# Padding the expert lists page by page during the token loop, and reading the expert rows back two tiles at a time

## What is computed

```python
x = x + attention(layernorm(x), ctx, valid_lens, Wq, Wk, Wv, Wo)
u = layernorm(x)
s = softmax(u @ centroids.T + expert_biases)
vals, idx = top_k(s, 2)                       # two experts a token
g = scatter(vals, idx)                        # 16 gates a token, 14 of them zero
routed = sum_e g[e] * (u @ Wr[e].T + br[e])
shared = (sum_n u @ Ws[n].T + sum_n bs[n]) / 2
out = x + u + routed + shared
```

## Time and profile before

| | us |
|---|---|
| median of 3 runs | 261.77 (260.43 to 262.01) |
| the profiled execution: its time | 261.29 |
| its span | 259.4 |

### The profile page before, as it was taken

The page is one execution under the profiler, slowest core; times in us unless marked ns, Lnnn a source line. Parts: engine busy times, 40 slices in busy tenths (PEclk is TensorE's granted clock), DMA queues, the critical chain, the costliest instruction groups (busy, mean ns, idle before and its releaser), DMA issues.

```text
span 259.4 us, 5036 instructions
## 1 busy us (share of the span) xinstructions
PE 219.6 (85%) x1530; PEld 184.8 (71%) x1530; DVE 152.5 (59%) x457; ACT 95.1 (37%) x241; POOL 106.3 (41%) x176
## 2 busy tenths in 40 slices
PE   7888999999999999999997943988669978576593
PEld 3767888888899998888875832867547757454482
DVE  1798778888888888888645930657503313140460
ACT  3114567566656666555442001222202213110022
POOL 1220222444444555444667200467566566574000
PEclk9999999999999999999999995999995999997689
DMA  6999990101011111100212693667455541200997
GB/s 170 361 247 373 426 414 16 43 20 44 20 44 41 43 41 44 42 22 27 79 39 71 159 206 100 201 197 221 137 169 163 172 130 36 90 17 9 332 382 248
DMA packets 20345, 36.30 MB, mean 140 GB/s; under 512 B 4059, under 2 KB 12765, under 8 KB 19936
## 3 DMA queue, kind: packets, MB, share of 16 engines
q1 hardware_dynamic: 13568, 22.50, 27.4%
q0 software_dynamic: 3792, 8.42, 9.2%
q10 hardware_dynamic: 2960, 5.07, 6.5%
HBM read 23.23 MB, written 14.71 MB: 146 GB/s over the span
## 4 chain that ended last, share of the span: by engine, by line
PE 67%; issue 9%; DMA 8%; DVE 4%; another core or an unknown queue 3%; SPq 3%; POOL 3%; ACT 1%; ACTq 1%; DVEq 0%; POOLq 0%
PE O L886 13%; PE T L808 7%; PE B L845 6%; PE B L953 5%; PE S L808 5%; PE A L808 4%; PE S L857 4%; PE B L1057 4%; PE T L1057 4%; PE A L1057 3%; DMA x<-in_x 3%; PE O L1057 3%; SPq L321 2%; PE S L1076 2%
## 5 line engine op out<-in xcount | busy, mean ns | idle before, releaser
L537 POOL DMA_INDIRECT lists<-urow,pos x32 | 32.8, 1024 | 41.6 <-PE S L857 34.0
L488 ACT ACTIVATE uTl<-S 128x256 f32<-128x256 f32 x47 | 17.0, 383 | 58.5 <-PE S L808 37.1
L415 ACT ACTIVATE pT<-T 128x512 f32<-128x512 f32 (+1 forms) x48 | 25.2, 526 | 30.4 <-PE T L808 28.7
L886 PEld LDWEIGHTS O<-vfront,pT 128*128 128x128 f32 x256 | 30.0, 192 | 0.1
L886 PE MATMUL O<-vfront,pT 128*128 128x34 f32 x256 | 29.9, 273 | 0.0
L665 DVE TENSOR_REDUCE rowmax<-S 128x16 f32<-128x1232 f32 x16 | 23.1, 1442 | 7.2 <-PE S L857 7.1
L568 POOL DMA_INDIRECT y<-yrow,padblock x16 | 15.8, 989 | 27.9 <-DVE yrow L786 20.7
L808 PE MATMUL T<-const,s_sb 128*128 128x128 f32 (+1 forms) x160 | 25.4, 273 | 2.0 <-DVE s_sb L680 1.2
L808 PEld LDWEIGHTS T<-const,s_sb 128*128 128x128 f32 (+1 forms) x160 | 19.1, 139 | 4.5 <-issue 2.7
L441 ACT ACTIVATE urow<-x,shift,rstds 128x256 f32<-128x256 f32 x32 | 19.1, 596 | 8.4 <-POOL shift L551 7.5
L680 DVE SCALAR_TENSOR_TENSOR s_sb<-S,rstds,scaledmax 128x1024 f32<-128x1024 f32 (+1 forms) x26 | 21.0, 850 | 0.0
(11 more groups left out here) (188 smaller groups left out, 432.7 us busy)
## 6 DMA issues: line engine op xcount, KB each, us to landing
padblock<-lists SPq DMA_DIRECT2D x32, 128.5 KB, 1.7
wr<-in_wrT SPq DMA_DIRECT2D x1, 4096.0 KB, 17.8
br<-in_br SPq DMA_DIRECT2D x1, 2048.0 KB, 21.9
wr<-y SPq DMA_DIRECT2D x8, 256.0 KB, 7.2
wr<-y ACTq DMA_DIRECT2D x8, 256.0 KB, 8.2
urow<-lists SPq DMA_DIRECT2D x15, 128.5 KB
xT<-in_xT SPq DMA_DIRECT2D x3, 512.0 KB, 7.7
x<-in_x SPq DMA_DIRECT2D x3, 512.0 KB, 8.0
```

The lines of the kernel that those rows point to most:

```text
L415: nc.scalar.activation(pT[t % 2][0:rows, c0:c1, :], T[0:rows, 0:c1 - c0, :], ACT.Exp).then_inc(p_ready, 1)
L537: nc.gpsimd.indirect_dma_start(out=lists, out_offset=bass.IndirectOffsetOnAxis(ap=pos[:, t, c:c + 1], axis=0), in_=urow[t % NR][c][:, :], ...
L886: last = M(to, pT[t % 2][0:v.shape[0], c, :], v.rearrange("p h j -> p (h j)"), start=(c == 0), stop=(c == CH - 1), skip_group_check=True)
```

## The change

Seven edits:

- `padblock` is filled whole: 16 rows of padding in each partition instead of 4.
- At the start, behind the same wait for `padblock`, SP writes padding over the first three pages (384 rows) of every expert's region, three DMAs of 2.1 MB, ahead of the loads of `x` and `xT` of tiles 8 to 15 (one DMA each now instead of two), `wr` and `br`. The first scatter waits for them (`filled`).
- In the steps of tiles 1 to 13, PE counts once more (`count_runs`, a product with one column), DVE works out with four small operations whether a list has reached a new page, and GpSimd issues an indirect DMA (`pad_page`) that writes the page three ahead of each list that has; for the others the row number lies outside and nothing is written. A partition holds one run of 16 rows, a page is 8 runs, 16 experts make the 128 partitions. `seen` becomes `seen_runs`, eight copies side by side.
- The scatter of tile t waits for the pad of tile t-2; SP waits for all pads before the first list load.
- `pad_lists` and `padrow` are gone from SP, ACT and DVE.
- `HANDOVER` is 12: the shared product of tiles 12 and 13 moves to the end as well.
- The y rows come in eight DMAs of two tiles (512 KB), 4 KB of a partition in one piece.

```diff
-HANDOVER = 14
+HANDOVER = 12
...
-        XGROUPS = [(0, 2), (2, 4), (4, 8), (8, 12), (12, 16)]
+        XGROUPS = [(0, 2), (2, 4), (4, 8), (8, 16)]
...
-            of = y_dram[b * SEQ * TOPK:(b + 1) * SEQ * TOPK, :].rearrange("(p t c) d -> t p c d", t=PER, c=TOPK)[t % PER]
-            eng.dma_start(ysum[:, t, :, :], of).then_inc(y_back[t], 16)
+            of = y_dram[b * SEQ * TOPK:(b + 1) * SEQ * TOPK, :].rearrange("(p t c) d -> p t c d", t=PER, c=TOPK)
+            eng.dma_start(ysum[:, t:t + 2, :, :], of[:, t % PER:t % PER + 2, :, :]).then_inc(y_back[t // 2], 16)
...
+            per_expert = lists[0:DUMMY, :].rearrange("(e n) w -> e n w", e=EXPERTS)
+            for page_of in range(REACH):
+                sp.dma_start(per_expert[:, page_of * P:(page_of + 1) * P, :].rearrange("e (b r) w -> e b (r w)", r=RUN),
+                             padblock[:, :, :].rearrange("p r w -> p (r w)")).then_inc(filled, 16)
...
-            pad_lists(sp, mybir.EngineType.SP, 0, EXPERTS // 2)
-            sp.wait_ge(table_ready, 2)
+            sp.wait_ge(table_ready, 1)
...
-                    sp.wait_ge(padded, 16 + 16 * EXPERTS)
+                    sp.wait_ge(filled, 16 * (1 + REACH))
+                    for i in range(2):
+                        sp.wait_ge(padded[i], 16 * len(range(1 + i, TILES - REACH + 1, 2)))
...
-            nc.gpsimd.memset(padblock[:, 0:PIECE, 0:D], 0.0)
-            nc.gpsimd.memset(padblock[:, 0:PIECE, D:ROW].bitcast(i32), PADROW).then_inc(pool_set, 1)
+            nc.gpsimd.memset(padblock[:, :, 0:D], 0.0)
+            nc.gpsimd.memset(padblock[:, :, D:ROW].bitcast(i32), PADROW).then_inc(pool_set, 1)
...
+                if t >= REACH:
+                    pool.wait_ge(padded[(t - REACH) % 2], 16 * ((t - REACH) // 2 + 1))
...
+            def pad_page(t):
+
+                pool.wait_ge(run_ready, t)
+                nc.gpsimd.indirect_dma_start(
+                    out=runs, out_offset=bass.IndirectOffsetOnAxis(ap=run_i[:, t:t + 1], axis=0),
+                    in_=padblock[:, :, :].rearrange("p r w -> p (r w)"), in_offset=None,
+                    bounds_check=DUMMY // RUN - 1, oob_is_err=False).then_inc(padded[(t - 1) % 2], 16)
...
+                    opens = 1 <= t <= TILES - REACH
+                    if opens:
+                        V.tensor_scalar(reached[:, :], run_bank(t), REACH * P - FRONT - 0.5, 1.0 / RUN, ALU.add, ALU.mult
+                                        ).then_inc(reached_ready, 1)
...
+                    if opens:
+                        dve.wait_ge(reached_ready, t)
+                        link(V.tensor_scalar(page[:, t:t + 1], reached[:, :], EIGHTS, EIGHTS, ALU.add, ALU.subtract))
+                        link(V.tensor_scalar(dropped[:, :], page[:, t - 1:t], page[:, t:t + 1], BEYOND, ALU.is_equal, ALU.mult))
+                        V.scalar_tensor_tensor(out=run_i[:, t:t + 1], in0=page[:, t:t + 1], scalar=cst("run"), in1=dropped[:, :],
+                                               op0=ALU.add, op1=ALU.add).then_inc(run_ready, 1)
...
+            def count_runs(t):
+
+                if 1 <= t <= TILES - REACH:
+                    M(run_bank(t), seen_runs[:, :, :].rearrange("p e b -> p (e b)"), ones16[:, 0:1], start=True, stop=True)
```

More of the change, by code:

```diff
@@ L41 @@
 FIRST = 3
+PARTS = P // EXPERTS
+RUN = P // PARTS
+REACH = 3
+BEYOND = 4096.0
+EIGHTS = 1.5 * 2.0 ** 26
 _COLS, _n = {}, 0
@@ L46 @@
                   ("resthead", HEADS // OCTS), ("before", P), ("expert", EXPERTS),
-                  ("upto", EXPERTS * EXPERTS), ("list", 1), ("listrow", 1), ("region", EXPERTS),
+                  ("upto", EXPERTS * EXPERTS), ("list", 1), ("listrow", 1), ("run", 1),
                   ("ids", TILES * TOPK)):
@@ L73, in _constants @@
     put("listrow", p[:, None] * P)
-    put("region", (e * REGION)[None, :])
+    put("run", (p // PARTS * (REGION // RUN) + p % PARTS)[:, None])
     t = np.arange(TILES)
@@ L182, in build @@
         start_i = sb("start_i", [LISTS, 1], i32)
-        padrow = sb("padrow", [1, EXPERTS], i32)
-        RUN, PIECE, NL, NY, NU = 16, 4, 24, 16, 4
+        reached = sb("reached", [P, 1])
+        page = sb("page", [P, TILES])
+        dropped = sb("dropped", [P, 1])
+        run_i = sb("run_i", [P, TILES], i32)
+        NL, NY, NU = 24, 16, 4
         padblock = sb("padblock", [P, RUN, ROW])
@@ L193, in build @@
         part = sb("part", [P, 2, D])
[L194 removed]
+        warm = part[:, :, :].rearrange("p a d -> p (a d)")
         diag = [pT[c][:, 0:HALF, :] for c in range(TOPK)]
@@ L252, in build @@
         shifted_ready = sem("shifted_ready")
-        padded = sem("padded")
+        filled, padded, run_ready = sem("filled"), [sem(f"padded{i}") for i in range(2)], sem("run_ready")
+        reached_ready = sem("reached_ready")
         l_arrived = [sem(f"l_arrived{j}") for j in range(NL)]
@@ L256, in build @@
         list_stepped, lT_ready, ly_ready = sem("list_stepped"), sem("lT_ready"), sem("ly_ready")
-        y_back = [sem(f"y_back{t}") for t in range(TILES)]
+        y_back = [sem(f"y_back{g}") for g in range(HALF)]
         part_ready, sum_ready = sem("part_ready"), sem("sum_ready")
@@ L310, in expert_column @@
                                   skip_runtime_bounds_check_because="the table keeps it at most the last expert")
[L312 to L322, removed]
         def list_load(eng, k, row):
@@ L381, in _ @@
                 sp.wait_ge(y_sent[j], 16 * len(range(j, LISTS, NY)))
-            for g in range(HALF):
-                load_y(sp, g)
+            for t in range(0, HALF, 2):
+                load_y(sp, t)
             for t in range(0, HALF, 2):
@@ L491, in _ @@
                 act.wait_ge(y_sent[j], 16 * len(range(j, LISTS, NY)))
-            for t in range(HALF, TILES):
+            for t in range(HALF, TILES, 2):
                 load_y(act, t)
@@ L505, in _ @@
             nc.gpsimd.memset(ones16[:, :], 1.0)
-            nc.gpsimd.memset(seen[:, :], 0.0).then_inc(pool_set, 1)
+            nc.gpsimd.memset(seen_runs[:, :, :], 0.0).then_inc(pool_set, 1)
             nc.gpsimd.memset(center[:, 1, :], -1.0 / D)
@@ L694, in take_shared @@
                                 x[:, 2 * i:2 * i + 2, :], ALU.add).then_inc(ws_taken, 2)
+            V.memset(page[:, 0:1], float((REACH - 1) * PARTS))
             dve.wait_ge(arrived["rest"], 16)
@@ L1031, in _ @@
             pe.wait_ge(out_taken, TILES)
-            M(B[:, 0:EXPERTS], ones16[:, :], seen[:, :], start=True, stop=False)
+            M(B[:, 0:EXPERTS], ones16[:, :], seen, start=True, stop=False)
             M(B[:, 0:EXPERTS], ones16[:, :], chosen[:, :], start=False, stop=True).then_inc(count_psum, 1)
```

36 lines of the change are left out of this document (22 added, 14 removed).

## The result

The changed kernel takes 265.67 us at the median of 15 executions (262.51 to 270.5), the kernel before 260.43 in the same session (259.81 to 262.97). The ratio is 1.0139, with a 95% interval of 1.0111 to 1.0166: slower by 1.4%.

A forecast was written before the change was run, and what follows sets the result against it. PE bounds the token loop, VectorE just as tight (0.06 us in hand); PE idles 7.73 us at the handover. Terms 2.6 + 1.5 + 6.7 - 8.2 + 0.7 = +3.3 on 261.3 give 264.6 us, range 258.3 to 269.

The forecast's parts named there:

- the largest term: Token loop: four more DVE operations lengthen ten steps by 0.65 us each, +6.5, plus 0.2 in the next: +6.7 us.
- the handover: Between token loop and lists: pads ahead of the first list load vanish, -8.2 us, ends -5 and -9.5.
- The rival by which the loop hides it: Token loop: DVE's added work is hidden, the 6.7 us vanish, 257.9 us; chance 0.13.
- the scatter of tile 15 waits for it, and may be 0.5 late: Loop's end: tile 13's pad opens two pages; the scatter waiting for it may come 0.5 us late.
- the rival of the late pad: Loop's end: tile 13's pad lands late, first list load some 3 us later, 267.6 us; chance 0.09.
- the pad of tile 12: Loop's end on GpSimd: this pad stands ahead of `vepss` of tile 15, +1.3 us, counted within the handover.
- the signs: What would show the forecast; here, at the loop's end, POOL's `vepss` follows the pad without a gap.
- The 0.8 us for the clock: Handover: without the hole PE's clock holds, first list multiply takes 1.0 instead of 2.07 us; 0.8 counted.
- `scaledmax` then ends near 17.4: Start: the longer padblock fill holds DVE's first `scaledmax`, which ends 2.6 us later.
- 4.1 was said: Start, to the first sum: +2.6 us for the whole padblock fill and +1.5 for PE's clock.
- the rival of 2.5 us: Token loop and its end: a pad costs GpSimd 2.5 us instead of 1.3, near 273 us; chance 0.10.
- The last stage was +0.7: After the lists: first sum and product wait for two tiles, 1.45 us later, partly showing; ends -0.5 and 1.5.

The follow-up runs named there:

- ops_only: Kernel before plus only three small VectorE operations like page, dropped and run_i ahead of the sum, results unused; ratio 1.0324 to the kernel before.
- after_again: The changed kernel profiled once more with no edit; ratio 1.0208 to the kernel before.
- spread: Changed kernel with each page's runs spread over the partitions instead of on eight neighbouring ones; ratio 0.9996 to the kernel before.
- after_third: The changed kernel, unedited, on another chip where the kernel before took 249.2 us; ratio 1.0207 to the kernel before.
- y_pairs: Kernel before with only the y loads changed, eight of two tiles instead of sixteen of one; ratio 0.9985 to the kernel before.
- sum_first: Changed kernel with page, dropped and run_i moved behind the sum that PE's queries wait for; ratio 0.9979 to the kernel before.

## Why the prediction was right, and where its terms were off

It said +3.3 us on 261.3, that is 264.6, in a range of 258.3 to 269; measured are 265.7, which is +3.6 by the ratio and +5.2 by the medians of all. The direction and the size are right, the mechanism of the largest term too. In the second pair of profiles, at +4.8, the handover was 3.6 us dearer than forecast (-4.6, not -8.2), the loop 0.4, and the start, the lists and the last stage together 2.5 cheaper. That the total came so near is in part luck.

**The loop was right.** `page`, `dropped` and `run_i` were put at 0.63 us together and measured 0.57 (7.99 to 7.43, and again in `ops_only`); `reached` and `seen_runs` at 0.02 and measured 0.09; the step at +0.65 and measured +0.65. It was eleven steps, not ten. What made this term exact was the row of PE's weight load ending 0.01 us before VectorE's sum: the kernel before had next to no room there. The rival by which the loop hides it falls.

**The handover was mis-sized.** The step that failed is "the scatter of tile 15 waits for it, and may be 0.5 late". GpSimd waited 2.5 to 4.04 us for that pad, and from the 14th sum to the last scatter it is 1.5 (`after_again`) to 3.5 us (the profile after) more than in `spread`, where nobody waits for it. This is the rival of the late pad, which had 0.09 and 3 us; it is what happened, near its size. The 0.5 had no row behind it, and a pad that opens two pages moves its 16 pieces from 16 partitions, packed, four at a time. Without that wait 1.7 us remain (23.8 in `spread`, 22.1 before), where 1.3 was said for the pad of tile 12. The list load came 3 us behind the last scatter, as said. `vepss` of tile 15 did not follow the pad of tile 12, as the signs had it, but the scatters of tile 13 (at 152.02, without a gap); the delay is the same. The 0.8 us for the clock did not come, since PE still waits for the first list (3.84 us in `after_third`) and its first multiply is at half clock again (2.02, 1.77 there).

**The start is two prices, and the first was over-sized.** "`scaledmax` then ends near 17.4" took the fill to begin at 13.83 as before; it began at 12.46 in the changed kernel and at 12.07 to 13.04 in others. So `scaledmax` lasted 2.12 us and not over 3, and PE's first transposes come at 17.2 to 18.2, 0.8 to 1.8 us later than before, where 2.6 was said. The clock then falls in six of the seven profiles with the late fill, not in `after_again`. Against the 27.62 of before the first sum is 1.0 us later where it holds, 2.5 to 3.5 where it is at half for 3.4 us, and 4.8 in `spread`, where it is so for 6.8 us; 4.1 was said. Against `y_pairs` (26.97) each is 0.65 more. That VectorE is held to the end of the fill was right; the rule quoted from the Trainium skill (SBUF — State Buffer, "Who interferes with whom") agrees with 2.0 to 2.7 us under the fill and 0.23 without it.

**A pad instruction costs GpSimd 1.0 us plus 0.3**, as said, though its rows are 16 KB; the rival of 2.5 us falls. **The fills cost nothing**: `x` of tiles 8 to 15 landed at 48.2, where 48 was said, and there is no wait for it in the loop, with 8.4 MB either. **The last stage was +0.7 and measured about 0** by `y_pairs`; in the two pairs of profiles it was +1.4 and -0.6. The reason was half right: the first product waits 1.3 us longer, but the time to the end is the same.

## What to carry to other kernels

Before a small operation is inserted, look at who waits for the next one on its engine: 0.57 us of VectorE work cost 6 us ahead of the operation that PE waits for and nothing 3.4 us later in the same step. A DMA that moves large pieces from a few neighbouring partitions was served here by a few DMA engines; lay the pieces out so that any subset is spread. And a fill on GpSimd belongs where VectorE has nothing to do that it could hold.

## What the runs showed of the hardware

- PE's clock falls in loops with short holes: with 0.54 to 0.64 us of idleness in each step of 8 us, PE busy 92 to 93% of the loop, the granted clock fell to half for 6.8 us in three of seven profiles, with no longer idleness in the loop ahead of it. Without the hole it fell in none of seven up to 125 us; in `sum_first` it fell at 131.5, behind an idleness of 0.83 us. Seven and seven profiles make this likely and do not prove it. The prediction looked for this only behind waits of 2 us and more.
- The level of a chip: the kernel before took 262.9 us on one chip and 249.3 on another. The token loop is the same on both; from the first to the last list multiply it is 70.2 us in `after_again` (69.5 in the profile of before) and 50.8 in that of `y_pairs`, where PE does not idle and GpSimd issues a scatter every 1.29 us. Of these 19 us 7 are lost again, since PE then waits for GpSimd's scatters and for y: from the last list multiply to ACT's last output it is 25.2 us before and 32.1 in `y_pairs`. What slows the list stage on the first was not tried.
